# A language-model tower in one launch: two heads in the two column halves of TensorE, one divided product for both, tables on ACT, preparation spread over the pair

## The chip, the cores and the metric

The kernel runs on one core of a Trainium2 chip. The metric is the device time of one execution in microseconds. The kernel before takes 3,328.92 us, the median of three runs (3,328.67 to 3,331.39).

## The reference

Inputs are two rows of 2,048 tokens. Everything is float32.

```python
h = weight.T[tokens] + bias                          # (2, 2048, 256)
x = layernorm(h)
xn = layernorm(x) * norm_g + norm_b
q = heads(xn @ Wq); k, v = heads(x @ Wkv)            # 16 heads of 64
k, v = [null_k, k], [null_v, v]                      # 2 null keys in front: 2050 keys
q, k = l2norm(q) * q_scale, l2norm(k) * k_scale
sim = 8 * q @ k.T - slope[head] * |j - i - 2|        # ALiBi, slope = 2 ** (-(head + 1) / 2)
attn = softmax(where(j > i + 2, -big, sim))          # causal
h = h + (attn @ v) @ Wout
y = layernorm(h)
w = top-2 of 8 experts by (y @ gate + lb_bias), sigmoid weights, divided by their sum
h = h + sum_e w[e] * (relu(y @ w1[e]) ** 2 @ w2[e]) + relu(y @ cfc) ** 2 @ cproj
```

## The kernel before

Work is cut by batch row (`NB` = 2) and by pair of heads (`NP` = 8): 16 head pairs `t`. Tokens come in 16 tiles of 128 (`T`), and query tiles in four groups `ig` of four tiles (`GW` = 512 queries). Scores are held transposed, keys on partitions and queries along the row.

**The blocks.** One head has 44 blocks (`BLKS`): group `ig` has 4 ig + 5 key tiles `jt`. The first 4 ig + 1 are 512 queries wide; the next are 386, 258 and 130, and the last one (two keys) is 2 wide. A pair has `PAIR` = 88 blocks `m`, head 0's 44 first. A block has four steps: `scores` (two fp16 products of a high and a low part, and a mask product on the diagonal) in one of two banks, `exp` on ACT into one of `PB` = 6 `probs` buffers, `sum_p`, which adds `probs` into `acc` on POOL or DVE, and `values`, the fp32 product with V, which gives 64 rows of output. `values` of even and odd blocks lie next to each other in the order. In groups 1 to 3 they write the two halves of one bank (`side(m)`: partitions 0 to 63 and 64 to 127), in group 0 both the first half.

**After a group.** `keep_o` copies the unnormalised output to `otf`. `sums` multiplies `acc` by ones; `keep_l` copies one row of the result, a DMA (`turn_l`) turns it into a column, and DVE's `inv_l` inverts it. `wout` multiplies 128 queries of `otf` by this head's 64 rows of Wout (held twice, for both halves), and DVE's `add_o` scales the product by the inverse and adds it to `h`. This is done for each head, group and tile: 32 `wout` a pair.

**The preparation of the next pair.** `proj` computes Q, K and V of one token tile; ACT's `square`, DVE's `ssq`, POOL's `inv_norm`, DVE's `unit` and POOL's `scale_k` normalise Q and K; `high`, `low`, `turn`, `keep` and a copy by DMA make the transposed fp16 parts. Then 44 units of `scores_a` and `max` find each query's maximum: `scores_a` computes high-part scores of both heads in two banks, and DVE adds an ALiBi table and takes the maximum. A product waits until both maxima of the unit before it are taken. `shift` and its followers put the maximum into the K = 65 product of `scores`. The ALiBi tables of a pair (`tables`) are written by POOL, ten instructions in one piece.

**What sets the order.** Each action gets a time in block units (`at(time, kind, ...)`), all are sorted, and every engine walks through its own actions in that order; an engine never overtakes. `SHARED` actions take two PSUM banks in turn, and one waits until the last but one user of its bank has been read (`RELEASE`). The front embeds batch 0, makes pair 0 ready and then starts its scores; the tail is the gate and nine experts for both batches.

Of the kernel before, what the change touches and what calls it, by code (L numbers as in the profile page):

```python
# [5 lines left out]
def lm_tower_kernel(nc, x, table, tok_bias, norm_g, norm_b, Wq, Wkv, q_scale, k_scale, null_kv, Wout,  # L6
# [20 lines left out]
    T = N // 128  # L27
# [29 lines left out]

    units = []
# [14 lines left out]
    def side(m):  # L73
        return m % 2 if blocks[m % BLKS][0] else 0
# [3 lines left out]
    DVE_SUMS = (2,)
    summed, so_far = [], [0, 0]
    for n in range(PAIRS * PAIR):  # L80
        on_dve = blocks[n % BLKS][0] in DVE_SUMS
        so_far[on_dve] += 1
        summed.append((on_dve, so_far[on_dve]))

# [18 lines left out]
    def project(t, t0, step):
        at(t0 - 60, "load_proj", t)
        at(t0 + 40, "load_out", t)
        for s in range(TK):
# [5 lines left out]
            at(s0 + 2.9, "unit", t, s)  # L112
            at(s0 + 3.0, "scale_k", t, s)
            if s == 0:
                at(s0 + 3.1, "null_v", t)
            if s % 2 == 1 or s == T:
                g = s // 2
                at(s0 + 4.2, "high", t, g)
                at(s0 + 5.0, "low", t, g)
                at(s0 + 6.0, "turn", t, g)  # L120
                at(s0 + 6.5, "keep", t, g)
                at(s0 + 6.6, "copy_low", t, g)

# [14 lines left out]
    def attend(t, t0):  # L138
        for m in range(PAIR):
            s0 = t0 + m - 0.9 * (m % 2)  # L140
            at(s0, "scores", t, m)
            at(s0 + 0.5, "exp", t, m)
            at(s0 + 1.4, "sum_p", t, m)
            at(t0 + (m | 1) + 1.9, "values", t, m)
        for hd in range(2):
            for ig in range(NG):
                e0 = t0 + ((hd * BLKS + last_block[ig]) | 1)
                at(e0 + 2.4, "keep_o", t, hd, ig)
                at(e0 + 2.6, "sums", t, hd, ig)
# [1117 lines left out]
```

## Time and the profile before

| | |
|---|---|
| median of three runs | 3,328.92 us |
| the profiled execution, its own time | 3,325.87 us |
| its span | 3,323.9 us |
| PE busy | 2,989.6 us, 90% |
| DVE busy | 2,013.1 us, 61% |
| ACT busy | 1,490.9 us, 45% |
| POOL busy | 1,631.9 us, 49% |
| granted TensorE clock, mean | 0.962 |

Times below are microseconds from the start of the span. L1146 is line 1146 of the kernel. A matmul's duration contains latency, so neighbours overlap; what one costs its engine is the distance between starts. "x4" after a group of matmuls in a timeline is that many records: an fp32 product has two for each call. The brackets at the end of a timeline row hold the idle time of the engine before it and what ended it.

### The profile page before, as it was taken

The page shows a single profiled execution, that of the slowest core. Times are in us where ns is not written, and L with a number is a line of the kernel's source. Part 1 is how long each engine was busy: PE and PEld are TensorE (multiplying, and loading weights), DVE is VectorE, ACT ScalarE, POOL GpSimd, SP SyncE. Part 2 cuts the span into 40 slices and gives each one's busy share as a digit, 9 for nine tenths or more (in the row PEclk, how much of TensorE's full clock was granted, in tenths as well). Part 3 has the DMA queues.
Part 4 walks back from the last instruction along what each step waited for, and adds up shares of the span by engine and source line. Part 5 has one row for each costly group of instructions (what it writes and reads, how often), then busy time and mean ns, then how long its engine had stood idle before and what let it go on. Part 6 is the DMA issues. An engine that isn't in the chain of part 4 may idle for free.

```text
span 3323.9 us, 50152 instructions
## 1 busy us (share of the span) xinstructions
PE 2989.6 (90%) x14241; PEld 1454.6 (44%) x14241; DVE 2013.1 (61%) x5648; ACT 1490.9 (45%) x2988; POOL 1631.9 (49%) x2152
## 2 busy tenths in 40 slices
PE   3589898989898987898989898989898989999999
PEld 2333434343434343434443434343434344666666
DVE  6666675666566658575757575756566663444444
ACT  3344555555555554555555555555555543111111
POOL 6454656565676564556565656565656543000000
PEclk9799999999999998999999999999999999999999
DMA  1000000000010000000000000000000100000000
GB/s 41 14 14 9 14 9 15 8 17 6 18 30 18 5 18 4 11 12 12 11 12 11 12 11 14 10 15 8 17 6 12 51 13 1 1 1 19 7 0 26
DMA packets 97495, 44.27 MB, mean 13 GB/s; under 512 B 38224, under 2 KB 96208, under 8 KB 97232
## 3 DMA queue, kind: packets, MB, share of 16 engines
q1 hardware_dynamic: 95696, 36.88, 4.3%
q0 software_dynamic: 1536, 4.20, 0.4%
q8 instruction: 127, 2.08, 0.3%
q14 instruction: 136, 1.11, 0.1%
HBM read 19.65 MB, written 4.19 MB: 7 GB/s over the span
## 4 chain that ended last, share of the span: by engine, by line
PE 63%; DVE 15%; POOL 11%; issue 9%; ACT 2%; DMA 0%; SPq 0%; DVEq 0%; POOLq 0%; ACTq 0%
PE ps L1146 13%; PE ps L1191 7%; PE ps L1204 7%; DVE ps L880 6%; PE ps L1130 5%; PE ps L1075 5%; PE ps L1163 5%; PE ps L1103 5%; PE ps L1131 4%; PE ps L1072 4%; PE ps L1153 3%; POOL rnorm L592 2%; POOL acc L628 2%; POOL tab_l L606 2%; DVE acc L915 1%
## 5 line engine op out<-in xcount | busy, mean ns | idle before, releaser
L715 ACT ACTIVATE probs<-ps,btab 128x512 f32<-128x512 f32 (+4 forms) x1408 | 768.3, 591 | 625.2 <-PE ps L1131 331.4
L628 POOL TENSOR_TENSOR acc<-acc,probs 128x512 f32<-128x512 f32 (+4 forms) x896 | 860.1, 960 | 162.6 <-ACT probs L715 84.3
L1146 PE MATMUL ps<-probs,arena 128*64 128x512 f32 (+4 forms) x2816 | 742.3, 530 | 0.0
L880 DVE CUSTOM_DVE_ANT_0 ps<-ps,tab_l 128x512 f32<-128x512 f32 (+1 forms) x896 | 568.2, 676 | 283.6 <-PE ps L1103 283.2
L1130 PE MATMUL ps<-arena 128*128 128x512 f16 (+4 forms) x1408 | 476.8, 339 | 0.7 <-issue 0.6
L1131 PE MATMUL ps<-arena 65*128 65x512 f16 (+9 forms) x1408 | 470.7, 336 | 0.0
L1163 PE MATMUL ps<-wo,otf 128*128 128x256 f32 (+1 forms) x1024 | 358.3, 432 | 5.6 <-DVE h L931 4.6
L931 DVE SCALAR_TENSOR_TENSOR h<-ps,rl,h 128x256 f32<-128x256 f32 x512 | 245.1, 479 | 132.0 <-PE ps L1163 131.5
L1103 PE MATMUL ps<-arena 64*128 64x512 f16 (+4 forms) x1408 | 256.7, 344 | 74.4 <-DVE mx L880 67.0
L592 POOL TENSOR_TENSOR rnorm<-nsq,minus_half 128x4 f32<-128x4 f32 (+1 forms) x272 | 298.3, 1097 | 22.7
L1072 PE MATMUL ps<-wqkv,xnT 128*128 128x128 f32 x1024 | 183.3, 304 | 136.0 <-DVE h L931 110.8
L989 DVE SCALAR_TENSOR_TENSOR h<-ps,wqkv,h 128x256 f32<-128x256 f32 x288 | 126.1, 480 | 295.6 <-PE ps L1204 295.6
L1075 PE MATMUL ps<-wqkv,xT 128*128 128x256 f32 (+1 forms) x1088 | 297.9, 399 | 0.0
L880 DVE CUSTOM_DVE_ANT_0 ps<-ps,tab_r 128x258 f32<-128x258 f32 (+2 forms) x512 | 207.7, 447 | 129.1 <-PE ps L1103 127.9
L1163 PEld LDWEIGHTS ps<-wo,otf 128*128 128x128 f32 (+1 forms) x1024 | 156.5, 190 | 294.2 <-issue 268.9
L589 POOL TENSOR_SCALAR nsq<-ssq 128x4 f32<-128x4 f32 (+1 forms) x272 | 80.9, 297 | 412.9 <-DVE ssq L844 412.7
L672 ACT ACTIVATE sq<-ps 128x256 f32<-128x256 f32 (+1 forms) x272 | 102.5, 377 | 396.5 <-PE ps L1075 394.7
L1146 PEld LDWEIGHTS ps<-probs,arena 128*64 128x64 f32 (+1 forms) x2816 | 181.5, 136 | 206.5 <-issue 143.3
L853 DVE TENSOR_TENSOR tqk<-raw,rnorm 128x256 f32<-128x256 f32 (+1 forms) x272 | 184.1, 677 | 136.3 <-POOL rnorm L592 136.1
L1204 PE MATMUL ps<-arena 128*128 128x256 f32 x1152 | 262.2, 379 | 4.3 <-DVE arena L979 4.3
L750 ACT ACTIVATE arena<-ps 128x1024 f32<-128x1024 f32 x72 | 73.7, 1024 | 405.7 <-PE ps L1191 405.7
L915 DVE TENSOR_TENSOR acc<-acc,probs 128x512 f32<-128x512 f32 (+4 forms) x384 | 226.4, 590 | 36.6 <-ACT probs L715 16.8
(128 smaller groups left out, 3753.7 us busy)
## 6 DMA issues: line engine op xcount, KB each, us to landing
arena<-arena SPq DMA_DIRECT2D x512, 32.0 KB, 1.9
wqkv<-in_Wkv SPq DMA_DIRECT2D x32, 128.0 KB, 2.4
wo<-in_Wout SPq DMA_DIRECT2D x64, 64.0 KB, 2.2
arena<-in_w SPq DMA_DIRECT2D x2, 2048.0 KB, 10.4
out<-h SPq DMA_DIRECT2D x8, 512.0 KB, 2.9
wqkv<-in_Wq SPq DMA_DIRECT2D x16, 128.0 KB, 2.4
arena<-augs SPq DMA_DIRECT2D x128, 1.0 KB
l_col<-arena SPq DMA_DIRECT2D x128, 2.0 KB, 2.0
```

The source lines that it names most:

```text
L592: pool.tensor_tensor(rnorm[0:rows, s % 2, c0:4], nsq[0:rows, s % 2, c0:4], minus_half[0:rows, c0:4], ALU.pow).then_inc(rnorm_ready, 1)
L628: pool.tensor_tensor(a, a, probs[0:rows, n % PB, 0:GW - c0], ALU.add).then_inc(sum_pool, 1)
L715: nc.scalar.activation(probs[0:rows, n % PB, 0:w], bank(S0 + n % 2)[0:rows, 0:w], ACT.Exp, bias=btab[0:rows, hh, z:z + 1]).then_inc(exp_do ...
L880: nc.vector.tensor_tensor_reduce(bank(A0 + hd)[:, 0:w], bank(A0 + hd)[:, 0:w], tab, 1.0, NEG, ALU.add, ALU.max, mx[:, hd, it, c:c + 1]).th ...
L1072: mm(o[:, 0:128], xnT[:, c, 128 * s:128 * s + 128], wqkv[:, r, c, 0:128], start=(c == 0), stop=(c == C - 1))
L1075: last = mm(o[0:rows, 128:384], xT[:, c, 128 * s:128 * s + rows], wqkv[:, r, c, 128:384], start=(c == 0), stop=(c == C - 1))
L1103: mm(bank(A0 + i)[:, 0:w], l[half, 0, i, 128 * it:128 * it + 128], l[half, 1, i, k0:k0 + w], start=True, stop=True).then_inc(a_ready, 1)
L1130: mm(dst[0:rows, 0:w], s[:, 1, hd, j], s[:, 0, hd, q], start=True, stop=False)
L1131: last = mm(dst[0:rows, 0:w], l[SPAN[hd], 1, hd, j], l[SPAN[hd], 0, hd, q], start=False, stop=not diag)
L1146: mm(bank(O0 + o % 2)[DH * z:DH * z + DH, c0:GW], vt[t % 2][0:rows, jt, hd, :], probs[0:rows, n % PB, 0:GW - c0], start=(jt <= (1 if ig el ...
L1163: mm(bank(z)[:, 0:D], otf[0:rows, o % 2, 128 * k:128 * k + 128], wo[0:rows, r, hd, :], start=True, stop=True).then_inc(w_ready, 1)
L1204: last = mm(bank(A0 + n % 2)[:, s * D:s * D + D], hid[:, i % 2, f, (2 * k + s) * 128:(2 * k + s + 1) * 128], w2s[:, e, f, :], start=(f == ...
```

## The change

- **Order of heads.** Block `m` is now head `m % 2`, block `m // 2` of the list. The two neighbouring `values` are the same block of both heads; head 0 goes to partitions 0 to 63 and head 1 to 64 to 127, in all groups.
- **End of a group.** `sums` writes both heads' sums in the two halves of one bank, each on 64 partitions. DVE's `divide` takes the reciprocal of 128x512 and multiplies the output by it into `otf`. One `wout` a tile has K = 128 for both heads (16 a pair), and `add_o` is a plain add. `keep_o`, `keep_l`, `turn_l` and `inv_l` go.
- **Sums.** DVE adds head 1 of group 3, POOL all else; in groups 1 to 3 the first add takes two `probs`; `acc` has three buffers.
- **Normalisation.** ACT copies Q and K straight to `tqk`; `unit` works in place in three instructions and takes the k scale along; `scale_k` goes.
- **Tables.** ACT writes them, eight instructions; DVE adds the mask.
- **Order in time.** `project` runs over 85 of the 88 units of the pair before (step 5.0, from PAIR t - 70), `maxima` from PAIR t - 34 to PAIR t + 48. Batch 1 is embedded with step 10. The front starts four gathers, then the constants; it clears the second arena later, and pair 0's maxima overlap with its first scores.

```diff
+    def block_of(m):
+        return (m % 2, *blocks[m // 2])
-    def side(m):
-        return m % 2 if blocks[m % BLKS][0] else 0
-    DVE_SUMS = (2,)
+    AB = 3
+    DVE_SUMS = ((NG - 1, 1),)
...
-            at(s0 + 2.9, "unit", t, s)
-            at(s0 + 3.0, "scale_k", t, s)
+            at(s0 + 2.6, "unit", t, s)
...
     def attend(t, t0):
         for m in range(PAIR):
...
-        for hd in range(2):
-            for ig in range(NG):
-                e0 = t0 + ((hd * BLKS + last_block[ig]) | 1)
-                at(e0 + 2.4, "keep_o", t, hd, ig)
-                at(e0 + 2.6, "sums", t, hd, ig)
-                at(e0 + 3.1, "keep_l", t, hd, ig)
-                at(e0 + 3.2, "turn_l", t, hd, ig)
-                at(e0 + 6.0, "inv_l", t, hd, ig)
-                for k in range(G):
-                    w0 = max(e0 + 6.3, wout_from[0] + 2)
+        for ig in range(NG):
+            e0 = t0 + 2 * last_block[ig] + 1
+            at(e0 + 2.6, "sums", t, ig)
+            at(e0 + 3.2, "divide", t, ig)
+            for k in range(G):
+                w0 = max(e0 + 5.3, wout_from[0] + 2)
...
-        at(-57 + 0.6 * u, "gather", 0, u)
-    embed(0, -51, 2.2)
+        at(-35 + (0.3 * u if u < 4 else 1.3 * (u - 4) + 1.9), "gather", 0, u)
+    embed(0, -31, 2.6)
...
-    project(0, -44, 1.6)
-    maxima(0, -17, 0.9)
+    at(-24, "zeros", 1)
+    project(0, -24, 1.6)
+    maxima(0, -14.4, 1.1, lambda g: -24 + 1.6 * (2 * g + 1) + 8)
     for t in range(1, PAIRS):
-        project(t, PAIR * (t - 1) + 1.6, 3.2)
-        at(PAIR * t - 66.5 if t > 1 else 27, "tables", t)
-        if t > 1:
-            maxima(t, PAIR * t - 59.5, 1.85)
-        else:
-            maxima(t, 32, 1.75)
+        project(t, PAIR * t - 70, 5.0)
+        maxima(t, PAIR * t - 34, 1.85)
     for t in range(PAIRS):
+        at(PAIR * t - 38 if t else -16, "tables", t)
         attend(t, PAIR * t)
...
-        embed(b, PAIR * (b * NP - 2) + 50, 3.8)
+        embed(b, PAIR * (b * NP - 1) - 62, 10)
...
+            def tables(t):                                   # on ACT
+                for hd in range(2):
+                    nc.scalar.activation(tab_l[:, hd, :], pos[:, 0:512], ACT.Copy, scale=slope).then_inc(tab_ready, 1)
+                    nc.scalar.activation(tab_r[:, hd, :], pos[:, :], ACT.Identity, bias=back[:, hh:hh + 1], scale=slope).then_inc(tab_ready, 1)
+                    nc.scalar.activation(tab_k[:, hd, :, :], key0[:, :, :], ACT.Copy, scale=slope).then_inc(tab_ready, 1)
+                    nc.scalar.activation(tab_g[:, hd, :], group_pos[:, :], ACT.Copy, scale=slope).then_inc(tab_ready, 1)
...
             def unit(t, s):
-                nc.vector.tensor_tensor(tqk[...], raw[...], rnorm[...].to_broadcast([rows, 2 - z0, 2, DH]), ALU.mult)
+                if s < T:
+                    nc.vector.tensor_tensor(q, q, rnorm[0:rows, s % 2, 0:2].unsqueeze(2).to_broadcast([rows, 2, DH]), ALU.mult)
+                for hd in range(2):
+                    last = nc.vector.scalar_tensor_tensor(out=k[:, hd, :], in0=k[:, hd, :], scalar=rnorm[0:rows, s % 2, 2 + hd:3 + hd],
+                                                          in1=scl[0:rows, :], op0=ALU.mult, op1=ALU.mult)
...
+            def divide(t, ig):
+                o = NG * t + ig
+                dve.wait_ge(l_ready, o + 1)
+                nc.vector.reciprocal(rl[:, :], shared_of("sums", t, ig)[:, :]).then_inc(rl_ready, 1)
+                dve.wait_ge(rl_ready, o + 1)
+                dve.wait_ge(pv_done, PAIR * t + 2 * last_block[ig] + 2)
+                need(dve, w_ready, G * (o - 1))
+                nc.vector.tensor_tensor(otf[:, o % 2, :], bank(O0 + o % 2), rl[:, :], ALU.mult).then_inc(o_read, 1)
...
-                nc.vector.scalar_tensor_tensor(out=h[:, b, it, :], in0=src[:, 0:D], scalar=rl[:, o % 2, k:k + 1],
-                                               in1=h[:, b, it, :], op0=ALU.mult, op1=ALU.add).then_inc(w_added, 1)
+                nc.vector.tensor_tensor(h[:, b, it, :], src[:, 0:D], h[:, b, it, :], ALU.add).then_inc(w_added, 1)
...
+            def sums(t, ig):
+                for hd in range(2):
+                    last = mm(bank(z)[DH * hd:DH * hd + DH, :], ones[:, :], acc[:, (2 * (NG * t + ig) + hd) % AB, :], start=True, stop=True)
...
+                mm(bank(O0 + o % 2)[DH * hd:DH * hd + DH, c0:GW], vt[t % 2][0:rows, jt, hd, :], probs[0:rows, n % PB, 0:GW - c0],
+                   start=(jt == 0), stop=(jt == G * ig + G)).then_inc(pv_done, 1)
...
-                mm(bank(z)[:, 0:D], otf[0:rows, o % 2, 128 * k:128 * k + 128], wo[0:rows, r, hd, :], start=True, stop=True).then_inc(w_ready, 1)
+                mm(bank(z)[:, 0:D], otf[:, o % 2, 128 * k:128 * k + 128], wo[:, r, :], start=True, stop=True).then_inc(w_ready, 1)
```

## Rows read from the trace of the kernel before

**Rows 1.** Busy us by stretch and engine: PE, PEld, DVE, ACT, POOL; clock; DMA.
```profile
0.00:346.00 346.00, 238.17 (x1149) 117.69 (x1149) 214.33 (x623) 137.41 (x310) 179.90 (x300) 0.89 0.08 19
548.30:711.70 163.40, 150.77 (x763) 67.08 (x763) 104.87 (x301) 85.56 (x174) 96.68 (x123) 0.97 0.05 12
1201.10:1397.60 196.50, 168.40 (x827) 77.25 (x827) 141.22 (x405) 102.17 (x222) 114.57 (x156) 0.92 0.04 10
2661.00:2793.00 132.00, 120.86 (x555) 51.52 (x556) 66.25 (x230) 60.74 (x110) 57.56 (x68) 0.94 0.01 3
```

**Rows 2.** Waits over the span: who for whom, us in total, times, longest us.
```profile
PE ps L1072 <- DVE h L931: 110.8, 28, 7.0
...
PE ps L1060 <- POOL slopes L545: 31.1, 1, 31.1
```

**Rows 3.** Timeline of PE, 540 to 553: start, us, what, idle before.
```profile
548.30 1.19 PE L1072 MATMUL ps<-wqkv,xnT 128*128 128x128 f32 x4 [6.95 <-DVE h L931]
```

**Rows 4.** Timeline of POOL, 537 to 549.
```profile
537.57 1.87 POOL L606 TENSOR_SCALAR tab_l<-pos,slopes 128x512 bf16<-128x512 f16 x1 [1.09 <-DVE aug L892]
...
545.20 0.79 POOL L612 TENSOR_TENSOR tab_r<-tab_r,mask_a 128x130 bf16<-128x130 bf16 x2
...
547.84 0.46 POOL L599 TENSOR_TENSOR tqk<-tqk,scl 128x128 f32<-128x128 f32 x1 [0.54 <-DVE tqk L853]
```

**Rows 5.** Timeline of DVE, 537 to 549.
```profile
547.34 0.42 DVE L853 TENSOR_TENSOR tqk<-raw,rnorm 128x256 f32<-128x256 f32 x1 [5.40 <-POOL rnorm L592]
```

**Rows 6.** Timeline of PE, 1569 to 1606: couples of values, `wout`, `sums`.
```profile
1569.78 1.27 PE L1146 MATMUL ps<-probs,arena 2*64 2x2 f32 x4
1570.98 1.05 PE L1153 MATMUL ps<-acc,ones 128*32 128x512 f32 x2
1571.96 0.62 PE L1087 MATMUL ps<-ident,blk 128*128 128x128 f16 x8
...
1577.36 1.08 PE L1146 MATMUL ps<-probs,arena 128*64 128x512 f32 x4
1578.37 0.70 PE L1163 MATMUL ps<-wo,otf 128*128 128x256 f32 x2
1578.90 0.61 PE L1072 MATMUL ps<-wqkv,xnT 128*128 128x128 f32 x4
...
1596.36 0.86 PE L1146 MATMUL ps<-probs,arena 128*64 128x386 f32 x4
1597.15 0.71 PE L1072 MATMUL ps<-wqkv,xnT 128*128 128x128 f32 x4
...
1599.85 0.64 PE L1146 MATMUL ps<-probs,arena 128*64 128x130 f32 x4
1600.42 0.39 PE L1103 MATMUL ps<-arena 64*128 64x512 f16 x2
...
1603.63 1.72 PE L1146 MATMUL ps<-probs,arena 128*64 128x512 f32 x4
1605.29 0.34 PE L1103 MATMUL ps<-arena 64*128 64x386 f16 x2
```

**Rows 7.** Groups of DVE, 548.3 to 711.7: xcount | busy us, mean ns | idle.
```profile
L880 DVE CUSTOM_DVE_ANT_0 ps<-ps,tab_l 128x512 f32<-128x512 f32 x48 | 32.3, 713 | 13.0 <-PE ps L1103 13.0
L931 DVE SCALAR_TENSOR_TENSOR h<-ps,rl,h 128x256 f32<-128x256 f32 x32 | 15.3, 478 | 7.4 <-PE ps L1163 7.4
...
L915 DVE TENSOR_TENSOR acc<-acc,probs 128x512 f32<-128x512 f32 x16 | 11.4, 710 | 1.1 <-ACT probs L715 0.3
L853 DVE TENSOR_TENSOR tqk<-raw,rnorm 128x256 f32<-128x256 f32 x16 | 11.2, 702 | 8.3 <-POOL rnorm L592 8.3
```

**Rows 8.** Groups of the whole span by form: reciprocals on DVE.
```profile
L967 DVE RECIPROCAL arena<-arena 128x128 f32<-128x128 f32 x2 | 1.9, 953 | 0.1
...
L971 DVE RECIPROCAL wsum<-wsum 128x16 f32<-128x16 f32 x2 | 0.5, 254 | 0.1
```

**Rows 9.** Groups of POOL, 548.3 to 711.7.
```profile
L628 POOL TENSOR_TENSOR acc<-acc,probs 128x512 f32<-128x512 f32 x32 | 41.0, 1281 | 6.6 <-ACT probs L715 3.7
```

More of the change, by code:

```diff
@@ L69, in lm_tower_kernel @@
     WR = 512 + NN
[L73 to L74 removed]
     PB = 6
[L78 removed]
+    AB = 3
+    DVE_SUMS = ((NG - 1, 1),)
     summed, so_far = [], [0, 0]
     for n in range(PAIRS * PAIR):
[L81 to L82 removed]
+        hd, ig, jt, _, _ = block_of(n % PAIR)
+        on_dve = (ig, hd) in DVE_SUMS
+        adds = jt > 0 or ig == 0
+        so_far[on_dve] += adds
         summed.append((on_dve, so_far[on_dve]))
+    for n in range(PAIRS * PAIR):
+        hd, ig, jt, _, _ = block_of(n % PAIR)
+        if jt == 0 and ig > 0:
+            summed[n] = summed[n + 2]
     plan = []
@@ L630, in _ @@
+                if ig == 0 and jt == 0:
+                    pool.tensor_copy(a, p).then_inc(sum_pool, 1)
+                else:
+                    first = ig > 0 and jt == 1
+                    pool.tensor_tensor(a, probs[0:rows, (n - 2) % PB, 0:GW] if first else a, p, ALU.add).then_inc(sum_pool, 1)
             for _, _, kind, which in plan:
@@ L644, in _ @@
                     inv_norm(*which)
-                elif kind == "scale_k":
-                    scale_k(*which)
-                elif kind == "tables":
-                    tables(*which)
         @block.scalar
@@ L902, in sum_p @@
                 n = PAIR * t + m
-                ig, jt, rows, c0 = blocks[m % BLKS]
-                o = (2 * t + m // BLKS) * NG + ig
+                hd, ig, jt, rows, c0 = block_of(m)
                 on_dve, count = summed[n]
-                if not on_dve:
+                if not on_dve or (ig > 0 and jt == 0):
                     return
-                a = acc[0:rows, o % 2, c0:GW]
+                i = 2 * (NG * t + ig) + hd
+                a = acc[0:rows, i % AB, c0:GW]
+                p = probs[0:rows, n % PB, 0:GW - c0]
@@ L923, in add_o @@
-            def add_o(t, hd, ig, k):
-                o = (2 * t + hd) * NG + ig
-                n = o * G + k
+                if jt == (1 if ig else 0):
+                    need(dve, l_ready, (i - AB) // 2 + 1)
+                if ig == 0 and jt == 0:
+                    nc.vector.tensor_copy(a, p).then_inc(sum_dve, 1)
+                else:
+                    first = ig > 0 and jt == 1
+                    nc.vector.tensor_tensor(a, probs[0:rows, (n - 2) % PB, 0:GW] if first else a, p, ALU.add).then_inc(sum_dve, 1)
@@ L1003, in _ @@
                     sum_p(*which)
-                elif kind == "inv_l":
-                    inv_l(*which)
+                elif kind == "divide":
+                    divide(*which)
                 elif kind == "ssq":
@@ L1112, in scores @@
             def scores(t, m):
-                hd, (ig, jt, rows, c0) = m // BLKS, blocks[m % BLKS]
+                hd, ig, jt, rows, c0 = block_of(m)
                 n, w = PAIR * t + m, GW - c0
```

262 lines of the change are left out of this document (111 added, 151 removed).

## The prediction

> **What bounds it now.** I read the busy time by stretches first [rows 1]. It splits the 3,323.9 us into a front with head pair 0 (to 346), fourteen steady pairs, the last pair (2,661 to 2,793) and the gate and expert tail. A steady pair takes 163.4 us: PE is busy 150.8 of them, DVE 104.9, POOL 96.7, ACT 85.6. The reader should see two things: PE carries the pair, and 12.6 us of it PE does not work. The tables run once a pair, so pair starts are one period apart, some 163 us; pair 7, beside which batch 1 is embedded, takes 196.5. In sum 346 + 13 x 163 + 196.5 + 132 + 531, which is the span within a us.
>
> Where the 12.6 us go is in the waits: PE's projection line waits for DVE's `add_o`, 110.8 us in 28 waits, longest 7.0 [rows 2]. The timeline has it once a pair, 6.95 us before 548.30 [rows 3]. POOL is at its `tables` from 537.57 to 545.99 [rows 4]; the inverse norm is behind them, DVE's `unit` waits 5.40 us for it [rows 5], `add_o` stands behind `unit`, and PE behind the bank that `add_o` frees. After it the first matmuls take nearly double: a pair of 512-wide values would be 1.08, the projections 0.71, and at 548.30 the line shows 1.19 [rows 3, 6]. The granted clock of the pair is 0.97, so part of it ran at 1.2 GHz and not at 2.4. I put that slow part at 2 us.
>
> **PE, part by part.** What one instruction costs PE is the distance from its start to the next start [rows 6]. A row of a couple of values names the form of its first member alone; the second's width follows from the block list.
> - Values. Two 512-wide products, one in each column half, take 1578.37 - 1577.36 = 1.01 us. In the same half (group 0 of a head, 512 and 386 wide) they take 1605.29 - 1603.63 = 1.66. A 2-wide and a 512-wide: 1.20. 386 and 258: 0.79. 130 and 2: 0.57. So a pair in two halves costs what its wider member costs, and the slope from 386 to 512 is 1.75 ns a column, which puts 258 wide at 0.57. Of a head's 22 couples now: 1.66; group 0's second one, same half, 388 columns at the 1.85 ns of the first, 0.72; two of 1.20; twelve of 1.01; two of 0.79; two of 0.57; (512, 386) 1.01; (258, 130) 0.57. That is 21.2, two heads 42.4. After, all 44 couples have equal widths: 28 of 1.01, four each of 0.79, 0.57, some 0.4 and some 0.35 (bounds for the last two 0.15 and 0.57): 36.7. Saved 5.7.
> - `wout`. 16 products a pair and not 32: 1578.90 - 1578.37 = 0.53 each, saved 8.5.
> - `sums`. Eight of 1571.96 - 1570.98 = 0.98 become four couples in two halves; I take them for 1.01, as values couples. Saved 3.8. If they did not overlap, nothing would be saved.
> - Scores, maxima products, projections, transposes: the same number, at other places.
>
> PE's work is 150.8 - 2 - 5.7 - 8.5 - 3.8 = 131 us a pair. That is the floor.
>
> **DVE.** Prices from [rows 7]. `add_o` 32 becomes 16 of 0.478: -7.7. Sums of one head of group 3 (12 adds and the small ones) for those of group 2 of both (16 adds, two copies, twice the small ones): about -5. `inv_l` (eight small reciprocals): -1. `unit` goes in place and takes the k scale along, three small instructions for one of 0.70: the nearest rows are half and whole of that one, so +0.2 x 16 = 3 (bounds 0 and 8). The mask add on `tab_r`: +0.5. `divide` is new: a reciprocal of 128x512 out of PSUM and a product of 128x512. No such reciprocal is in the trace; 128x16 takes 254 ns and 128x128 953 [rows 8], 6.24 ns an element, so 953 + 384 x 6.24 = 3.35 us. The product I take as the 0.71 of a 512-wide add [rows 7]. Four times 4.06 is 16.2 (bounds: 12, if the slope flattens, 20, if PSUM makes it dearer). DVE's total is 104.9 - 13.7 + 3.5 + 16.2 = 111, up 6.
>
> **POOL and ACT.** POOL loses tables (8.4 us [rows 4]) and `scale_k` (16 of about 0.46 and one small one [rows 4], 8) and gains four wide adds of 1.28 [rows 9]: 96.7 - 16.4 + 5 = 85. ACT loses eight row copies of the sums and eight copies of the product and gains eight table instructions: below 85.6 in any case, and both have slack in 140 us. With that the 6.95 us wait and the slow 2 us go: what held `unit` up is no longer on POOL. The tables now stand between exps on ACT, eight instructions in one piece (bounds: the 8.4 us that POOL takes, and nothing); PE has two score banks, and I take 1.5 us lost there. POOL's four more adds cost nothing while exps come slower than POOL sums them: two heads' adds are 2.56 us [rows 9] against some 3 us of PE for two blocks.
>
> **The new wait.** `divide` is 4.06 us in one piece, four times a pair. Behind it on DVE are `unit`, `low`, `add_o`, and the maxima; PE's next maxima products need both maxima before them, the next `wout` needs the quotient. In the new order `sums` is at e0+2.6 block units, the next maxima product a unit or two later, the first `wout` at e0+5.3. Between `sums` and `wout` PE has about four scores, one values couple and one maxima product, some 3 us. DVE finishes the two maxima that it is at (2 x 0.71 [rows 7], of which `sums` hides most) and then divides: PE stands 1 to 2 us at `wout`. The next maxima come behind it and cost 1.4 to 2 more. Together 2 to 4 us, less where the units are short: I take 3, so 12 a pair. Nearly nothing (0.5 each) to 6 each are the bounds. For other short waits, the table burst included, 2 us remain of the 5.7 that are there now beside the long one. A steady pair: 131 + 12 + 2 = 145 us, 18 less than before.
>
> **Front.** PE does nothing for its first 31 us [rows 2]: DVE clears both arenas, POOL issues 16 gathers and then writes constants before the roots. DVE is busy 214 of 346 us [rows 1]. The change clears one arena later, sends four gathers first and lets pair 0's scores start while its later maxima are still made. DVE's work up to the end of pair 0 becomes about 230 (pair 1's maxima are done less far by then); at 85% busy that is 270. I take 275, saved 71 (bounds 20 and 100).
>
> **Pair 7, last pair, tail.** Embedding adds 36 us of DVE and took 33 us [rows 1]; spread over 80 units beside a DVE at 76%, I give it 22: 167. The last pair, 132, has all the values, `wout` and sums (-18) but new stalls (+9) and loses its overhang of maxima (-8): 115. The tail keeps its work; the last divide stands bare: 531 + 2.
>
> **Sum.** 275 + 13 x 145 + 167 + 115 + 533 = 2,975 of span, 2,977 on the profiled execution's own count (3,325.9, which is 2 more than its span); the median of the runs shown is 3 above that: 2,980 us.
>
> **Rivals.**
> - DVE, not PE, sets the pair. For it: pair 7 now, where 36 us more of DVE made the pair 33 longer with DVE busy only 72% [rows 1], so in this order DVE counts long before it is full; 111 us at that share would be 154. Against it: there the extra work came in one lump. Price: 154 to 158 a pair, 10 to 13 more on 13 pairs, 3,110 to 3,150. Chance 0.25.
> - The divides are absorbed: PE has other products queued, DVE catches up, and the pair is 134. Speaks for it: `add_o` and `sums` lighten DVE elsewhere. Against: the static order. 275 + 13 x 134 + 160 + 110 + 533 = 2,820. Chance 0.2.
> - Slower than before: each divide stops PE until DVE has worked off all that is queued. A pair at the floor saves 32 us; front, pair 7 and last pair save some 115, which is 8 more for each of 14 pairs. So the stall would have to be above 10 us a divide, two and a half times its own length. At 12 us a divide it would be 3,326 + 14 x 4 x 2 = 3,440. Chance 0.03.
> - The products in two heads' halves do not overlap (PE saves only `wout`): 9.5 us more a pair, about 3,100 with the stalls as forecast. Against it: couples of one head overlap now, in the same bank. Chance 0.04.
> - The forecast, 2,880 to 3,060: chance 0.48.
>
> **Range.** From the absorbed case to the DVE-bound one: 2,820 to 3,130. Within 0.2% (7 us, about what a measurement here can tell from no change) 0.01, slower 0.04, faster 0.95.
>
> **What would show it.** In the profile after: 512 `wout` records for 1,024; values couples of group 0 at 1.01; a reciprocal of 128x512 near 3.35 us; no 6.95 us wait before the projections; PE waiting at `wout` for the product of `divide` and at the maxima products for DVE, together some 12 us a pair; first matmul before 31 us. Wrong it would be if the reciprocal took twice that, if PE stood longer than 5 us at a divide, or if its clock fell at each of them.

## The result and the profile after

The changed kernel takes 3,425.39 us (median of four runs, 3,422.47 to 3,428.19) beside 3,328.8 for the kernel before in the same session. The ratio is 1.0291, 95% interval 1.0273 to 1.0309: slower, by 2.9%. The forecast was 2,980 us, range 2,820 to 3,130. Sign and range were both missed.

The page of the kernel after, engine totals:

```profile
PE 2829.8 (83%) x13729; PEld 1419.9 (41%) x13729; DVE 2313.0 (68%) x5792; ACT 1333.8 (39%) x2860; POOL 1460.9 (43%) x1765
```

PE has 160 us less to do than before, and the kernel is 97 us longer. DVE has 300 us more. The windows of the kernel after, for the front with pair 0, a steady pair, and the last pair (the columns are those of [rows 1]):

```profile
0.00:292.50 292.50, 198.63 (x1029) 101.63 (x1029) 205.12 (x578) 123.90 (x290) 152.69 (x220) 0.89 0.09 21
1617.40:1791.40 174.00, 141.86 (x730) 65.47 (x730) 125.14 (x311) 75.78 (x166) 85.59 (x100) 0.90 0.04 10
2746.00:2892.00 146.00, 122.18 (x594) 52.48 (x595) 101.10 (x284) 54.02 (x111) 68.31 (x81) 0.87 0.11 34
```

Beside [rows 1] a steady pair is 10.6 us longer, 174.0 for 163.4. In it PE is busy 9 us less and idle 32.1 us, where it was idle 12.6; the granted clock is 0.90 for 0.97. Pair 7 takes 190.8. So 292.5 + 13 x 174 + 190.8 + 146 + 534 = 3,425, the span of 3,425.9.

These windows cut the front and the last pair at another place of the pair than [rows 1] did. Counted by first exps, which is the same place in both kernels, the time up to pair 1's is 46 us shorter (285.4 for 331.9), the 13 steady pairs have a mean of 174.1 for 162.9, pair 7 takes 190.8 for 196.4, and the last pair, from its first exp to its last, 142.1 for 135.7. The steady pairs lose 146 us, and everything else together wins 44.

Who PE waits for in this steady pair (waits view):

```profile
PE ps L1084 <- DVE mx L854: 18.8, 11, 2.9
PE ps L1091 <- DVE aug L866: 5.9, 2, 5.5
PE ps L1111 <- ACT probs L689: 3.1, 1, 3.1
PE ps L1147 <- DVE otf L901: 2.2, 2, 1.3
PE ps L1091 <- DVE h L909: 1.4, 1, 1.4
```

L1084 is `scores_a`, L1091 `turn_shift`, L1111 `scores`, L1147 `wout`. The wait at `wout` is 2.2 us a pair. Nearly 19 us stand in front of the maxima products. The long wait of [rows 3] is gone, and eleven short ones and a new long one have its place.

The groups of DVE in the same pair:

```profile
L854 DVE CUSTOM_DVE_ANT_0 ps<-ps,tab_l 128x512 f32<-128x512 f32 x48 | 32.2, 710 | 5.7 <-PE ps L1084 5.5
L827 DVE SCALAR_TENSOR_TENSOR tqk<-tqk,rnorm,scl 128x64 f32<-128x64 f32 x32 | 15.7, 531 | 0.0
L825 DVE TENSOR_TENSOR tqk<-tqk,rnorm 128x128 f32<-128x128 f32 x16 | 13.5, 842 | 8.6 <-POOL rnorm L583 8.6
L897 DVE RECIPROCAL rl<-ps 128x512 f32<-128x512 f32 x4 | 13.4, 3358 | 0.6 <-PE ps L1137 0.4
...
L892 DVE TENSOR_TENSOR acc<-acc,probs 128x512 f32<-128x512 f32 x11 | 11.0, 1004 | 0.9 <-ACT probs L689 0.9
L909 DVE TENSOR_TENSOR h<-ps,h 128x256 f32<-128x256 f32 x16 | 6.7, 418 | 8.0 <-PE ps L1147 7.9
L814 DVE TENSOR_REDUCE ssq<-sq 128x4 f32<-128x256 f32 x16 | 6.7, 416 | 19.8 <-ACT sq L645 19.8
```

The reciprocal is 3.36 us, as worked out. But `unit` (L825, L827) is 29.2 us where it was 11.2 [rows 7], although it has no more elements. The part with half of the columns takes 842 ns in the mean and each of the parts with a quarter 531, where the whole took 702. And DVE, busier than before, stands idle 19.8 us in front of `ssq`. In the kernel before it was 11.1 (waits view of the pair of [rows 7]):

```profile
DVE ssq L844 <- ACT sq L672: 11.1, 6, 3.5
```

The longest wait in the timelines, DVE, POOL and PE:

```profile
1612.53 1.35 DVE L825 TENSOR_TENSOR tqk<-tqk,rnorm 128x128 f32<-128x128 f32 x1 [3.35 <-POOL rnorm L583]
1613.81 1.47 DVE L827 SCALAR_TENSOR_TENSOR tqk<-tqk,rnorm,scl 128x64 f32<-128x64 f32 x2
...
1616.56 0.82 DVE L866 TENSOR_TENSOR aug<-tab_g,rowmax 128x8 f16<-128x8 f32 x1
```
```profile
1611.46 1.04 POOL L583 TENSOR_TENSOR rnorm<-nsq,minus_half 128x4 f32<-128x4 f32 x1
1612.47 2.72 POOL L602 TENSOR_TENSOR acc<-acc,probs 128x512 f32<-128x512 f32 x2
```
```profile
1617.44 0.27 PE L1091 MATMUL ps<-ident,aug 128*8 128x128 f16 x1 [5.49 <-DVE aug L866]
```

DVE idles 3.35 us for the inverse norm, `unit` then lies under two POOL adds and takes 2.8 us, and the last step of the shift, for which PE stands, is behind it. Further on, DVE and ACT under the two next waits of PE (2.86 us before 1638.41, 3.06 before 1627.00):

```profile
1633.40 3.36 DVE L897 RECIPROCAL rl<-ps 128x512 f32<-128x512 f32 x1
1636.79 0.69 DVE L901 TENSOR_TENSOR otf<-ps,rl 128x512 f32<-128x512 f32 x1
1637.40 0.42 DVE L854 CUSTOM_DVE_ANT_0 ps<-ps,tab_r 128x258 f32<-128x258 f32 x1
```
```profile
1623.06 0.71 ACT L700 ACTIVATE tab_l<-pos,slopes 128x512 bf16<-128x512 f16 x1
...
1626.59 1.23 ACT L689 ACTIVATE probs<-ps,btab 128x130 f32<-128x130 f32 x4
```

A `divide` holds the maxima for 4.0 us, and the eight table instructions hold the exps for 3.5.

The products did what was forecast. PE's timeline:

```profile
1735.65 0.65 PE L1147 MATMUL ps<-wo,otf 128*128 128x256 f32 x2
1736.23 1.08 PE L1127 MATMUL ps<-probs,arena 128*64 128x512 f32 x4
1737.24 0.23 PE L1084 MATMUL ps<-arena 64*128 64x130 f16 x2
```

A values couple of both heads costs 1737.24 - 1736.23 = 1.01 us, and there are 512 `wout`, 16 a pair.

### The profile page after: what moved, and what is told of

It is laid out like the page before. It is cut to its first block, busy times and chain, and to the rows that moved or that the text cites. A ratio compares the mean times of both kernels' runs of the same rounds, so it can differ in the third digit from the quotient of the medians.

```text
span 3425.9 us, 47657 instructions
## 1 busy us (share of the span) xinstructions
PE 2829.8 (83%) x13729; PEld 1419.9 (41%) x13729; DVE 2313.0 (68%) x5792; ACT 1333.8 (39%) x2860; POOL 1460.9 (43%) x1765
## 4 chain that ended last, share of the span: by engine, by line
PE 39%; DVE 21%; POOL 19%; issue 17%; ACT 4%; POOLq 0%; DMA 0%; ACTq 0%; DVEq 0%
POOL acc L602 12%; PE ps L1188 7%; PE ps L1175 7%; DVE rl L897 5%; DVE ps L854 5%; PE ps L1056 5%; POOL rnorm L583 4%; PE ps L1127 4%; DVE tqk L827 4%; PE ps L1111 3%; DVE tqk L825 3%; PE ps L1084 3%; PE ps L1112 3%; PE ps L1053 2%; ACT probs L689 2%
## 5 line engine op out<-in xcount | busy, mean ns | idle before, releaser
L1127 PE MATMUL ps<-probs,arena 128*64 128x512 f32 (+4 forms) x2816 | 652.4, 541 | 0.0
L1111 PE MATMUL ps<-arena 128*128 128x512 f16 (+4 forms) x1408 | 504.4, 360 | 49.1 <-ACT probs L689 47.8
L1084 PE MATMUL ps<-arena 64*128 64x512 f16 (+4 forms) x1408 | 248.8, 346 | 306.4 <-DVE mx L854 300.6
L1112 PE MATMUL ps<-arena 128*128 128x512 f16 (+9 forms) x1408 | 495.8, 354 | 0.0
L1056 PE MATMUL ps<-wqkv,xT 128*128 128x256 f32 (+1 forms) x1088 | 366.5, 471 | 0.0
L1084 PEld LDWEIGHTS ps<-arena 64*128 64x128 f16 x1408 | 74.9, 93 | 643.3 <-issue 640.0
L814 DVE TENSOR_REDUCE ssq<-sq 128x4 f32<-128x256 f32 (+1 forms) x272 | 110.5, 406 | 290.1 <-ACT sq L645 282.3
L825 DVE TENSOR_TENSOR tqk<-tqk,rnorm 128x128 f32<-128x128 f32 x256 | 203.5, 795 | 131.7 <-POOL rnorm L583 131.5
L1111 PEld LDWEIGHTS ps<-arena 128*128 128x128 f16 (+1 forms) x1408 | 144.3, 103 | 344.9 <-ACT probs L689 138.8
L827 DVE SCALAR_TENSOR_TENSOR tqk<-tqk,rnorm,scl 128x64 f32<-128x64 f32 (+1 forms) x544 | 249.1, 496 | 0.0
L1188 PEld LDWEIGHTS ps<-arena 128*128 128x128 f32 x1152 | 220.2, 192 | 65.8 <-issue 33.6
L1056 PEld LDWEIGHTS ps<-wqkv,xT 128*128 128x128 f32 (+1 forms) x1088 | 229.6, 234 | 33.0 <-issue 2.8
```

The costliest lines, as they stand in the source:

```text
L825: nc.vector.tensor_tensor(q, q, rnorm[0:rows, s % 2, 0:2].unsqueeze(2).to_broadcast([rows, 2, DH]), ALU.mult)
L827: last = nc.vector.scalar_tensor_tensor(out=k[:, hd, :], in0=k[:, hd, :], scalar=rnorm[0:rows, s % 2, 2 + hd:3 + hd], in1=scl[0:rows, :], ...
L1056: last = mm(o[0:rows, 128:384], xT[:, c, 128 * s:128 * s + rows], wqkv[:, r, c, 128:384], start=(c == 0), stop=(c == C - 1))
L1084: mm(bank(A0 + i)[:, 0:w], l[half, 0, i, 128 * it:128 * it + 128], l[half, 1, i, k0:k0 + w], start=True, stop=True).then_inc(a_ready, 1)
L1111: mm(dst[0:rows, 0:w], s[:, 1, hd, j], s[:, 0, hd, q], start=True, stop=False)
L1112: last = mm(dst[0:rows, 0:w], l[SPAN[hd], 1, hd, j], l[SPAN[hd], 0, hd, q], start=False, stop=not diag)
```

## The experiments

Eighteen kernels; line 14 holds two. 11 and 15 have four times each, the others one, and the four times of a kernel lie within 0.4% of each other. A pair is the distance between the first exps of two neighbouring head pairs, of one steady pair or the mean of two to four neighbours; the mean of all steady pairs lies within 1.3 us of it, but in run 16 at 158.7. Idle is the pair less PE's busy time. Runs 1, 2, 16 and 17 leave a part of the work out, as is said at each. The diffs show the main lines only.

| kernel | us | pair | PE busy | idle | clock |
|---|---|---|---|---|---|
| before | 3,328.8 | 163.4 | 150.8 | 12.6 | 0.97 |
| after | 3,425.4 | 174.0 | 141.9 | 32.1 | 0.90 |
| 1 reciprocal of 16 columns | 3,196.5 | 160.4 | 137.3 | 23.1 | 0.91 |
| 2 one `unit`, no k scale | 3,282.7 | 163.8 | 138.0 | 25.8 | 0.93 |
| 3 tables apart | 3,397.3 | 173.2 | 142.0 | 31.2 | 0.90 |
| 4 before, tables on ACT | 3,240.3 | 157.3 | 149.4 | 7.9 | 0.99 |
| 5 one `unit`, k scale on POOL | 3,330.4 | 167.2 | 140.1 | 27.1 | 0.92 |
| 6 reciprocal on ACT | 3,192.1 | 158.9 | 136.9 | 22.0 | 0.93 |
| 7 3, 5 and 6 together | 3,046.2 | 148.8 | 132.4 | 16.4 | 0.96 |
| 8 old times | 3,193.2 | 158.0 | 135.6 | 22.4 | 0.95 |
| 9 old times, projections only | 3,235.3 | 160.6 | 135.1 | 25.5 | 0.95 |
| 10 6 and 8 | 2,975.8 | 143.2 | 130.3 | 12.9 | 0.98 |
| 11 7 and 8 | 2,902.6 | 138.7 | 128.9 | 9.8 | 0.99 |
| 12 7 and 9 | 2,904.3 | 139.1 | 129.6 | 9.5 | 0.98 |
| 13 step 3.2 from - 70 | 3,143.2 | 153.6 | 132.7 | 20.9 | 0.97 |
| 14 step 4.1 / step 4.9 | 3,222.1 / 3,332.7 | 160.6 / 167.6 | 139.3 / 140.0 | 21.3 / 27.6 | 0.92 / 0.92 |
| 15 7 with 13 | 2,985.0 | 144.1 | 132.0 | 12.1 | 0.96 |
| 16 POOL writes, reads nothing | 3,190.5 | 156.0 | 135.6 | 20.4 | 0.94 |
| 17 `unit` in four | 3,460.1 | 177.3 | 143.7 | 33.6 | 0.89 |

**Runs 1 to 4: the suspects of the prediction.**

```diff
# 1
-                nc.vector.reciprocal(rl[:, :], shared_of("sums", t, ig)[:, :]).then_inc(rl_ready, 1)
+                nc.vector.reciprocal(rl[:, 0:16], shared_of("sums", t, ig)[:, 0:16]).then_inc(rl_ready, 1)
...
# 2 (unit)
...
+                nc.vector.tensor_tensor(qk, qk, rnorm[...].to_broadcast([rows, 2 - z0, 2, DH]), ALU.mult).then_inc(qk_read, 1)
...
# 3
-        at(PAIR * t - 38 if t else -16, "tables", t)
+        for i in range(8):
+            at(PAIR * t - 40.4 + 0.9 * i if t else -16 + 0.01 * i, "tables", t, i)
```

1: 

> The changed kernel with the reciprocal of divide taken over 16 of the 512 columns; the other 496 columns of rl keep the value 1 written at the start, so the division is left out there. Theory A (the 3.36 us reciprocal, four times a pair, is what PE waits for at the maxima products and at wout, about 14 of the 32 us of waits, and the clock falls after those waits): the pair falls from 174 to about 157 and the kernel to 3,150 to 3,220 us. Theory B (DVE is held back by POOL: unit waits for the inverse norm and for POOL's adds, and the reciprocal only fills time that DVE would wait in anyway): the kernel stays above 3,350 us.

2: 

> The changed kernel with unit as one instruction over Q and K in place, as before; the multiplication by the k scale is left out. Theory A (reciprocal): 14 us less of DVE work a pair but the same waits at divide, so at most 60 us less, above 3,360. Theory B (three instructions that read two SBUF tensors each stand behind a POOL add where there was one; the trace has 0.28 us for one that meets no POOL instruction and 0.65 to 0.89 for one that does): the chain unit, low, shift becomes 1.5 to 3 us shorter at each of 17 steps, pair 174 to about 163, kernel 3,230 to 3,290 us.

3: 

> The changed kernel with the eight table instructions on ACT 0.9 block units apart, between the exps, instead of in one piece of 4.1 us. If the piece costs what the wait behind it shows, 3.06 us and some slow clock after it, 14 times: 3,360 to 3,385 us. If the wait only moves to the next maximum or shift: 3,410 to 3,430 us.

4 (the kernel before, its tables by ACT 0.75 units apart, the mask by DVE): 

> The kernel before with one part of the change: the tables on ACT (spread, 0.75 units apart), the mask added by DVE. If POOL's tables are the cause of the 6.95 us wait and of the slow clock behind it, once in each of 14 pairs, and nothing takes their place: 9 us a pair less, 3,190 to 3,220 us. If the wait for the DMA that turns the sums, or POOL's other work, takes its place: 3,280 to 3,330 us.

Measured 3,196.5, 3,282.7, 3,397.3 and 3,240.3 us. Without the reciprocal's length a pair is 13.6 us shorter, with one `unit` 10.2, with the tables apart one to three (its steady pairs take 170.7 to 174.4). And the one part of the change that takes POOL's tables away is worth 88 us on the kernel before: its long wait [rows 3] goes, and the pair's idle time falls from 12.6 to 7.9.

**Runs 5 to 7: each cost mended without leaving work out.** In 5 `unit` is one product in place and POOL scales k again. In 6 the reciprocal is exp(-ln(x)) on ACT, and the product that is left of `divide` comes 0.8 units later (not in these lines):

```diff
+                nc.scalar.activation(rl[:, :], shared_of("sums", t, ig)[:, :], ACT.Ln).then_inc(l_read, 1)
+                act.wait_ge(l_read, o + 1)
+                nc.scalar.activation(rl[:, :], rl[:, :], ACT.Exp, scale=-1.0).then_inc(rl_ready, 1)
...
-                nc.vector.reciprocal(rl[:, :], shared_of("sums", t, ig)[:, :]).then_inc(rl_ready, 1)
```

5: 

> The changed kernel with this part undone: unit is one instruction (in place) and the k scale is multiplied by POOL's scale_k again. The one-instruction unit without the k scale gave 3,282.7 us (pair 163.8). Theory (DVE's three locked instructions cost more than POOL's 0.48 us hop): 3,290 to 3,320 us. Rival (the longer chain to high and low gives it back, since low stands in DVE's queue): above 3,380 us.

6: 

> The changed kernel with the reciprocal made on ACT as exp(-ln(sum)), two 128x512 instructions of some 0.65 us each, so that of divide only the 0.69 us product is left on DVE. With the reciprocal over 16 columns the kernel took 3,196.5 us (pair 160.5). Theory (what costs is the 3.36 us in one piece on DVE): 3,200 to 3,240 us. Rival (the two instructions on ACT hold up exps, or table loads are put between them, 1.3 us each): above 3,300 us.

7: 

> All three at once on the changed kernel: reciprocal on ACT, unit in one instruction with scale_k on POOL, tables spread. If the three costs add up (13.5, 9 and 2.5 us a pair of 174): pair 149, kernel 3,030 to 3,080 us. If they overlap, since behind each stands the same DVE: 3,100 to 3,180 us.

Measured 3,330.4, 3,192.1 and 3,046.2. The two ACT instructions take 597 and 630 ns where DVE's took 3,358, and the gain is that of run 1. Together the three parts give 379 us, 23 more than their sum alone (95 + 233 + 28), so they don't hide one another. What the k scale costs on POOL is the 48 us between runs 2 and 5.

**Runs 8 and 9: the order in time.** I had costed it at nothing.

```diff
-        project(t, PAIR * t - 70, 5.0)
-        maxima(t, PAIR * t - 34, 1.85)
+        project(t, PAIR * (t - 1) + (1.6 if t > 1 else 10), 3.2)
+        if t > 1:
+            maxima(t, PAIR * t - 58, 1.85)
+        else:
+            maxima(t, 44, 1.45)
```

8 puts tables and the second embedding back too (not in these lines). 9 puts back projections and embedding alone. The times are those of the kernel before but for small shifts in the maxima and in pair 1.

8: 

> The changed kernel with the order in time of the kernel before for projections, maxima, tables and the second embedding (project from 1.6 with step 3.2, maxima from -58). Theory (the waits come from DVE's pieces, not from the spread): the same or slower, 3,420 to 3,520 us, since DVE has less room beside the projections. Rival (the spread order is what costs, it puts a maxima unit next to every divide): below 3,380 us.

9: 

> The changed kernel with projections and the second embedding at the times of the kernel before; maxima and tables stay where the change put them (maxima from PAIR t - 34). The old order of all three took 232 us off. If it is the spreading of the projections that costs (a short wait in front of each of 17 token tiles, over the whole pair), this run gets most of it: 3,190 to 3,250 us, steady pair 157 to 162. If it is the place of the maxima, which now end half way through the pair that uses them, with group 1's and group 2's divides among them, little is gained: 3,370 to 3,425 us, pair 171 to 174. Both in equal parts would be some 3,300.

8 measured 3,193.2 us: my expectation fell and the rival's held. The order costs 232 us, as much as the reciprocal. 9, at 3,235.3, has 190 of them: it is the projections. Of the other 42, 16 are at the very end: from its first exp to its last, the last pair takes 142.1 us after, 135.5 in 9 and 119.9 in 8. With the new times the last pair's maxima run on to its 46th unit and not to its 22nd. The rest is in the pairs before. The projections reach into the pair that uses them too: with PAIR t - 70 and step 5.0 the last three of the 17 tiles begin at its units 0, 5 and 10, so they don't all lie in the pair before, as "The change" has it.

**Runs 13 and 14: which thing about the projections' times.** All begin at PAIR t - 70. In 13 the step is 3.2, in 14 it is 4.1 and 4.9, after has 5.0. With 3.2 and 4.1 batch 1's embedding is at its old times.

```diff
-        project(t, PAIR * t - 70, 5.0)
+        project(t, PAIR * t - 70, 3.2)
```

13: 

> The changed kernel with the projections packed as before (step 3.2 for 5.0) but begun where the change begins them (PAIR t - 70), and the second embedding at its old times. With step 3.2 begun 16 units earlier it took 3,235 us, with step 5.0 begun here 3,425. If the spreading is what costs (more short products each with a wait before it beside all of the pair, and so a lower clock), this run is near 3,235: 3,220 to 3,270. If the beginning is what costs (which divides and maxima the projections meet), it is near 3,425: 3,370 or more.

14, step 4.9: 

> The changed kernel with the projections' step 4.9 for 5.0, nothing else. With 5.0 every token tile stands at the same place between the score blocks, with 4.9 no two do. If the fixed place is what the spread projections lose by, a good part of the 282 us that step 3.2 gave comes with it: 3,150 to 3,330 us. If it is the spreading itself, it is the changed kernel again: 3,400 to 3,430.

14, step 4.1: 

> Half way between the changed kernel (step 5.0, 3,425 us) and the packed one (step 3.2, 3,143): step 4.1, begun at the same place, the second embedding early. If the cost grows with the spreading: 3,260 to 3,310 us. If any step but 5.0 would do: 3,143 to 3,200. If only the packed one is good: above 3,370.

Measured 3,143.2 (3.2), 3,222.1 (4.1), 3,332.7 (4.9), 3,425.4 (5.0). A tenth of a unit in the step is worth 93 us, a third of the 282. The next steps bring 111 and 79. That the first third comes from the fixed place of the tiles between the blocks fits the numbers, but is not shown: with 4.9 PE's 7.3 us a pair before L1091 are 2.0, 5.1 us of new waits for `blk` stand elsewhere, and in all PE idles 4.5 us less. No run keeps the step at 5.0 and moves the start by a part of a unit, which would tell a fixed place from this fixed place. Whether the rest goes by the packing, by a luckier place, or by tiles that no longer begin in the pair that uses them, these runs don't tell either. The moved embedding is not it: 13 steady pairs that are 20.4 us shorter make 265 of the 282. The window of run 13:

```profile
1537.00:1690.60 153.60, 132.72 (x731) 60.80 (x730) 125.29 (x311) 76.10 (x166) 83.48 (x100) 0.97 0.04 11
```

DVE is busy 125.3 us as after, with the same instructions, and the pair is 20.4 us shorter. PE idles 11.2 us less, and its own work is 9.1 us less at a clock of 0.97 for 0.90. So DVE's total alone did not set the pair; the order in which it was done counts. The waits of DVE and PE in that pair, for 19.8 and 18.8 us after:

```profile
DVE ssq L814 <- ACT sq L645: 4.2, 2, 2.3
PE ps L1084 <- DVE mx L854: 12.5, 12, 2.4
```

**Two more: does `unit` wait for POOL?**

```diff
# 16, POOL's adds write ones and read nothing
-                    pool.tensor_tensor(a, probs[0:rows, (n - 2) % PB, 0:GW] if first else a, p, ALU.add).then_inc(sum_pool, 1)
+                    pool.memset(a, 1.0).then_inc(sum_pool, 1)
# 17, unit in four products with one input from SBUF each
+                    last = nc.vector.tensor_scalar(k[:, hd, :], k[:, hd, :], rnorm[0:rows, s % 2, 2 + hd:3 + hd], None, ALU.mult)
```

16: 

> The changed kernel with POOL's adds of probabilities replaced by a write of ones to the same place: POOL reads nothing there (the sums are left out). The three instructions of unit took 842, 531 and 531 ns in the mean after, 272 and 269 where no POOL instruction ran beside them. If they wait for POOL's reads of SBUF, the ones beside such a write take the short times, and the group's means fall to 350 and 320 or less, and the 128x512 add on DVE from 1,004 to about 700. If it is any POOL instruction that they wait for, or the reciprocals and maxima beside them on DVE, those with a write beside them stay long. The time: unit's excess of some 15 us a pair was worth 9 to 10 us a pair in the run without it; POOL's earlier end of the inverse norm adds to that: 3,200 to 3,290 us. If POOL's length is without effect, 3,290 or more.

17: 

> The changed kernel with unit as four products of 64 columns by one value per partition, so that each has one input from SBUF (the k scale is left out). If the two inputs are what makes unit wait for POOL, these take 0.12 to 0.2 us each with or without POOL beside them, 0.5 to 0.8 a tile instead of 1.9, and the time is that of the run with one product in place, or less: 3,230 to 3,290 us. If any DVE instruction on SBUF waits, or many short ones are dear, unit stays at 1.5 to 2 us a tile and the time at 3,400.

Run 16 took 3,190.5 us, 10 below what was expected. Its groups of DVE in a pair:

```profile
L827 DVE SCALAR_TENSOR_TENSOR tqk<-tqk,rnorm,scl 128x64 f32<-128x64 f32 x32 | 7.6, 278 | 0.0
L892 DVE TENSOR_TENSOR acc<-acc,probs 128x512 f32<-128x512 f32 x11 | 7.5, 685 | 0.9 <-ACT probs L689 0.9
...
L825 DVE TENSOR_TENSOR tqk<-tqk,rnorm 128x128 f32<-128x128 f32 x16 | 4.6, 288 | 6.1 <-POOL rnorm L583 6.1
```

531 became 278 ns, 842 became 288, 1,004 became 685. Over the whole run 192 of L825's instructions had a POOL write beside them, and the longest of those took 294 ns; in the kernel after the 206 that had a POOL add beside them took 918 in the mean, up to 1,366. So it is POOL's reads that they wait for, and not POOL's instructions as such. DVE's busy time in a pair is 104 us for 125. POOL's own instructions are shorter too (49 us a pair for 86), so the 235 us of the kernel's time are not the price of the reads alone.

Run 17 fell: 3,460.1 us, with

```profile
L827 DVE TENSOR_SCALAR tqk<-tqk,rnorm 128x64 f32<-128x64 f32 x32 | 15.7, 529 | 0.0
L825 DVE TENSOR_SCALAR tqk<-tqk,rnorm 128x64 f32<-128x64 f32 x32 | 15.2, 516 | 8.5 <-POOL rnorm L583 8.5
```

One tensor input did not free them: alone such an instruction takes 242 to 246 ns, beside an add on POOL 561 (L825) and 657 (L827) in the mean. The Trainium skill has both on "SBUF — State Buffer", section "Who interferes with whom": a DVE instruction with two SBUF inputs contends with a GpSimd (POOL) one that reads SBUF, not with one that only writes; and `tensor_scalar` may use both ports for one tensor and can then contend too. The traces agree with the first, 918 ns beside an add and 289 beside a write. For the second they show the waiting, but not its way: the value per partition is read from SBUF as well.

**Runs 10 to 12 and 15: the best of it.** `unit`, reciprocal, tables mended, and each of the orders.

10: 

> The changed kernel with the reciprocal on ACT (exp of minus ln) and with the order in time of the kernel before. Alone each took some 232 us off 3,425. Theory 1, they remove different costs (DVE's length, and what stands in front of PE's short products): the sum, 2,960 us, pair 140. Theory 2, both remove the same stalls (DVE late for PE), the rest is PE's own work with the slow clock: 3,080 to 3,120 us, pair 150 to 153.

11: 

> Everything that helped at once: reciprocal on ACT, unit in one product with the k scale on POOL, tables' instructions spread, and the old order in time. Beside the same kernel in the new order (3,046 us, pair 148.5). Theory 1, the order costs stalls of its own: PE at the predicted 131 to 135 us of work and few waits, pair 138 to 142, 2,900 to 2,960 us. Theory 2, with DVE at 100 us of work the order matters no more: 3,030 to 3,060 us, pair 148. Rival with the other sign: POOL's tail of sums and k scale in the denser order holds up DVE, 3,080 us.

12: 

> As the kernel with everything at once in the old order, but with the maxima and the tables where the change put them: only projections and the second embedding at the old times. If the spread projections are what the order costs, it is as fast as that kernel to within 20 us and the maxima's place costs nothing; if the maxima's place costs, it stays near 3,046 us.

15: 

> Reciprocal on ACT, unit in one product with the k scale on POOL, tables' instructions spread, and projections with step 3.2 begun at PAIR t - 70. In the changed kernel this beginning was 92 us better than the old one at the same step. If the same holds here: 2,810 to 2,870 us for the 2,904 of the kernel with the old projections. If the cost was stalls behind the divides and unit, which this kernel does not have, it is the same: 2,890 to 2,915.

10 is the sum to within 16 us (2,975.8 for 2,960). 11 takes 2,902.6 us, four runs from 2,899.39 to 2,911.23, ratio to before 0.8720, interval 0.8706 to 0.8735: 12.8% faster than the kernel before, 15.3% faster than the kernel after. Its pair:

```profile
1429.80:1568.50 138.70, 128.93 (x731) 59.24 (x730) 99.67 (x274) 80.33 (x174) 90.54 (x117) 0.99 0.05 13
```

12 equals it, so the place of the maxima and tables costs nothing there. 15 fell: 2,985.0 us, ratio 0.8975 (0.8958 to 0.8993). Both of my cases had it at 2,915 or less. The start at - 70 that was 92 us better than the old one in the changed kernel is 81 us worse once DVE's pieces are short; why, no run shows. An order in time is good or bad for given durations, not by itself.

## Why the prediction was wrong

**The floor held.** 131 us of PE work were forecast. It is 132.7 at a clock of 0.97 (run 13) and 128.9 at 0.99 (run 11). Values couples, `wout`, sums in two halves are worth what the prices said. So are the prices of the reciprocal (3.36 for 3.35; the 4.3 set beside it did not come), its product (0.69 for 0.71), `add_o` (0.42 for 0.48), POOL's 85 us and the tail's 533. The rival in which the two heads' halves don't overlap is out.

**The step that failed is "131 + 12 + 2", and in it the 2.** Of the 29 us that the pair is over 145, 18 are idle time of PE (32.1 for 14) and 10.9 are its own work at the lower clock. "For other short waits, the table burst included, 2 us remain": with the reciprocal cut to 16 columns (run 1) PE still idles 23.1 us a pair. And "DVE's total ... 111, up 6" was 125.1, up 20. Two causes were missing.

**The order in time was costed at nothing in the steady pair.** The prediction let the projections move and asked only what stood behind the divides. Each of the 17 tiles has a chain from PE over ACT, DVE, POOL and back to DVE, and on every engine its links stand in a fixed line. Spread over the pair, the tiles put DVE in front of an unready `ssq` eight times a pair, for 19.8 us; in the packed order of run 13 it is twice, 4.2 us. The wait before `unit` is no part of it: 8.3 us before, 8.6 after, 10.4 in run 13. In the same pair the maxima products wait 12.5 us for DVE and not 18.8. Packing took 20.4 us off the pair and 282 off the kernel. That DVE comes to `ssq` later, because more is queued before it, and that this is why the maxima are less late, is argued and not shown. What stays open is the rule: the best place in the changed kernel is not the best with short DVE pieces (run 15).

**"+0.2 x 16 = 3 (bounds 0 and 8)" for `unit` was wrong: it is +18** (29.2 for 11.2). The term was set by halves of the row of [rows 7], 702 ns for 256 columns. That mean held waits for POOL already: in the kernel before such an instruction takes 419 ns with nothing on POOL beside it and 930 beside an add. And the wait doesn't shrink in proportion to the instruction: beside an add, 64 columns (L827) lose 0.40 us in the mean, 128 (L825) 0.63, 256 0.51 to 0.75 (before, runs 2 and 5), 512 (L892) 0.60. Three instructions a tile wait more than one. Not all of the 18 is the splitting: the one product of run 5 takes 977 ns in the mean, 15.6 us for the 16 of a pair (the row below has 17), so 13.6 come with the splitting and 4.4 without it. Without POOL's reads `unit` is 12.2 us, near the forecast 14.2. Its price in the time is 95 us (run 5) with POOL doing the k scale, 143 with the scale left out (run 2).

```profile
L835 DVE TENSOR_TENSOR tqk<-tqk,rnorm 128x256 f32<-128x256 f32 x17 | 16.6, 977 | 10.4 <-POOL rnorm L585 10.4
```

**The divides cost about what was taken.** 12 us a pair were forecast; making the reciprocal 16 columns took 13.6 off the pair, 9.0 of it idle time and 4.6 PE's slow work, and 229 us off the kernel. "Nearly nothing to 6 each" holds: 3.4 each. 1 to 2 us were expected at `wout` for each divide and 1.4 to 2 at the maxima products. At `wout` it is 2.2 for all four. In front of the maxima products there are 18.8 a pair, of which 7.7 are the reciprocal's, since run 1 leaves this (its lines are numbered one higher):

```profile
PE ps L1085 <- DVE mx L855: 11.1, 10, 2.9
```

**The slow clock.** 2 us of slow work were to go. Instead the work at a clock of 0.90 is 141.9 us, where run 11 does the same products in 128.9 at 0.99. In the table the clock goes roughly with the idle time: 31 us and more idle, 0.89 or 0.90; 20 to 28, 0.91 to 0.97; below 17, 0.96 to 0.99. Between after and run 13, 11.2 us less idle time came with 9.1 less work. But the idle total alone doesn't set it: two steady pairs of run 16 that both idle 20.6 us ran at 0.90 and 0.95, with 140.0 and 134.3 us of work. So no fixed price of slow work for a us of waiting follows.

**Table burst:** 1.5 us forecast, 3.1 in the wait, 28 us in the kernel. **Front:** 292.5 for 275, forecast 18 too short: DVE has 205 us there and not 230, but is busy 70% and not 85%. **Pair 7:** 190.8 for 167, but 17 over a steady pair for the forecast 22, so that term held. **Last pair:** 146 for 115: "loses its overhang of maxima (-8)" had the sign wrong. The maxima run over 46 units of the pair that uses them, where before they ran over 22. Maxima and tables at the old times take 16 us off that pair (run 9 to 8), the projections and the embedding 7 (after to run 9).

Of the rivals, "slower" had 0.03, with a stall of over 10 us a divide. The outcome was on its side and the mechanism was not: no divide stalls PE 10 us. "DVE sets the pair" took 111 us at 72% busy for 154. At the 125.1 us that DVE turned out to have, the same share gives 174, the pair measured. But the same work takes 153.6 us in run 13, at 82%, so that share is no bound. In the changed order DVE's work did count: 13.1 us less of it in run 6 came with a pair 15.1 shorter. In the sum the error was to price each engine's work and one new wait, and to take the rest of the waits for 2 us because they had been small in another order.

## What to carry to other kernels

In a program whose engines each walk a fixed line, a move in time is a change like any other: price every link of the moved chain, and when unsure move it by a tenth of a step and look, since 0.1 units were worth 93 us here. Don't split an instruction on DVE that waits for POOL: read its shortest and its mean duration first, and take the difference as a price nearer to one per instruction than to one per element. When a kernel becomes slower by a bundle of edits, undo them one at a time: with the order taken back, `unit` and tables mended and the reciprocal on ACT, this bundle is 12.8% faster than the kernel before.

## What the hardware showed

- DVE instructions of 64 to 512 columns on SBUF take up to 1.1 us more beside a POOL add that reads SBUF: a `tensor_tensor` of 128 columns takes 285 ns alone, 918 in the mean beside an add, up to 1,366, and 289 beside a POOL write. `scalar_tensor_tensor` of 64 columns has 274 and 674, fp32 `tensor_scalar` of 64 columns 242 to 246 and 561 to 657.
- A reciprocal of 128x512 fp32 from PSUM takes 3.36 us on DVE; ln and then exp of it on ACT take 0.60 and 0.63.
- Two fp32 products in the two column halves of one bank take the time of one: 1.01 us for twice 512 columns, where one product of `sums` took 0.98 [rows 6], also when they belong to different sums.
